# Down products of ten units in three feed-forwards as float32r passes, with their low parts made by GpSimd

## The chip, the core and the metric

One Trainium2 chip, one of its cores. The metric is the device time of one launch in microseconds, first to last instruction plus a little around it. Three runs of the kernel before gave 507.08, 507.49 and 510.03 us, median 507.49.

## What is computed

Sixteen sequences of 128 tokens with 256 channels go through two layers. The first is a WKV recurrence over the tokens and then a feed-forward with a product-key mixture of experts beside it; the second is a linear cross attention and then a mixture of eight experts with the best two per token. What the change touches is the first feed-forward, cut from the reference:

```
mlp = silu(x @ gate_w) * (x @ up_w) @ down_w          # 256 -> 1024 -> 256
ew  = silu(einsum('nh,nkh->nk', x, de)) * softmax(scores)
experts_states = einsum('nk,nkh->nh', ew, ue)         # 512 experts, 8 chosen by keys
x = x + tanh(g_ffn[0]) * (mlp + experts_states)
```

## The kernel before

All 2048 tokens stay in SBUF. They are worked on in four groups of four sequences (512 tokens, `GN`). Each group has one feed-forward, ("mlp", 0) to ("mlp", 3), here called the first to the fourth. A feed-forward has twelve units of 128 hidden rows: eight of the dense part and four of the experts of the product keys. For each unit TensorE makes the hidden rows (`block_up`: for a dense unit banks A and B, six float32r matmuls of 512 columns each, since the product of two float32 values is made as low times high, high times low, high times high), ScalarE takes Silu of A into the ring `act_s` of four buffers, VectorE multiplies with B, and TensorE multiplies the result with the unit's rows of `w_down` (`down`, L678: four token tiles, one float32 matmul of 256 columns each, added up in the two banks `acc`). A float32 matmul stands in the trace as two records, a float32r matmul as one.

The order of the whole program is one list, `SCHED`, written by hand, and every engine walks it in the same order and does its share of each step. A feed-forward has the parts 1 to 13 (and the downs of units 10 and 11 as parts 14 and 15); part p makes the hidden rows of unit p-1 and the down product of unit p-4 (`LAG` is 3), and after it stand the steps of other work that the table `PLAN` gives for that part: the recurrence of later groups (`wkv_in`, `wkv_out`), keys and values of the attention (`kv_k`, `kv_e`, `kv_v`), the routing of the experts (`route`), and from the third feed-forward on the attention (`attn`) and the second layer's experts (`moe`, `place`, `rows`, `send`). No engine goes past an instruction that waits. TensorE takes the six PSUM banks `ring` in turn, so it can run ahead of the engines that empty them by six banks.

Places that matter below. The step `clear` of the second feed-forward's part 12: after the last keys GpSimd zeroes a row in `v_t0`, and SyncE copies it over the tensors `x_rows` in HBM by two large DMAs (L1756, semaphore `rows_cleared`). The step `send`: GpSimd scatters rows that ScalarE scaled (`rows`, L1158) by indirect DMAs (L1677), two per tile. `wkv_out 3 3` and `3 5`: GpSimd multiplies with the reciprocals of VectorE (L1655). Memory is full: the names in `with nc.sbuf_tensor(...)` and `pass` are second names for words of what is allocated behind them.

## Time and profile before

| | |
|---|---|
| median of 3 runs | 507.49 us |
| profiled execution | 508.22 us |
| its span, first to last instruction | 506.4 us |
| granted TensorE clock, mean | 0.974 of full |
| TensorE, VectorE, ScalarE, GpSimd busy | 89%, 69%, 49%, 34% |
| first feed-forward's downs begin | 66 us |
| third and fourth feed-forward | about 207 to 385 us |

The span is 1.8 us shorter than the time of the same execution; that rest lies around the program. The engines of the table overlap, so their shares don't add. Stages are told apart by the start of the down products: those of the second feed-forward run from 144.8 to 206.4 us, those of the third from 221.8 to 298, those of the fourth from 319 to 384. In a timeline a row may hold several instructions of one kind ("x8"); the bracket at its end is the idle time of the engine before it and what ended that.

### The profile page before, as it was taken

To read this page: it belongs to the slowest core of one execution; us is meant where nothing else is said; L and a number is where in the kernel's file an instruction comes from. 1 tells how busy PE (TensorE), PEld (TensorE's weight loads), DVE (VectorE), ACT (ScalarE), POOL (GpSimd) and SP (SyncE) were. 2 spreads that over 40 slices of the span, in tenths; PEclk is the share of its full clock that TensorE was granted. 3 is DMA by queue.
4 is the path that set the end of the run, shared out by engine and by line. 5 is a ranking of instruction groups with operands and counts; after the bars stand their busy time and mean duration, and the time that the engine had idled before them with its cause. 6 is when DMAs were issued, how large, how long until landed. Compare 5 with 4: busy or idle time off the path is not lost. (4 is left out here: it accounts for less than half of the span.)

```text
span 506.4 us, 7287 instructions
## 1 busy us (share of the span) xinstructions
PE 450.3 (89%) x2162; PEld 356.1 (70%) x2162; DVE 347.2 (69%) x994; ACT 247.2 (49%) x479; POOL 173.8 (34%) x181
## 2 busy tenths in 40 slices
PE   2769799589989999999999998998998899899991
PEld 1447588458668776888778786887776688788860
DVE  6968569988486964577978967888778354621173
ACT  2868264223577377455044416360751544955540
POOL 3787232354022333400000000060525015477771
PEclk9999799789999999999999999999999899999997
DMA  8421212002000000980000000142323223346494
GB/s 306 164 80 57 62 33 80 5 20 83 1 1 2 0 1 0 293 218 0 1 2 1 0 2 0 32 136 74 119 71 112 88 79 111 105 150 191 123 380 138
DMA packets 32966, 42.02 MB, mean 83 GB/s; under 512 B 3483, under 2 KB 26781, under 8 KB 32928
## 3 DMA queue, kind: packets, MB, share of 16 engines
q1 hardware_dynamic: 28224, 32.28, 21.0%
q0 software_dynamic: 3744, 8.42, 4.5%
q10 hardware_dynamic: 960, 0.86, 0.5%
q8 instruction: 19, 0.31, 0.3%
q14 instruction: 19, 0.16, 0.1%
HBM read 24.97 MB, written 18.39 MB: 86 GB/s over the span
## 5 line engine op out<-in xcount | busy, mean ns | idle before, releaser
L678 PE MATMUL acc<-w_down,act_s 128*128 128x256 f32 x384 | 91.5, 384 | 0.9 <-DVE act_s L1410 0.9
L678 PEld LDWEIGHTS acc<-w_down,act_s 128*128 128x128 f32 x384 | 73.6, 193 | 12.8 <-DVE act_s L1410 1.3
L654 PE MATMUL ring<-xt_h,up_l 128*128 128x512 f32 x160 | 71.1, 444 | 1.4 <-DVE kv_sum L1490 1.4
L1137 ACT ACTIVATE act_s<-ring 128x512 f32<-128x512 f32 x48 | 28.6, 596 | 73.5 <-PE ring L656 73.3
L655 PE MATMUL ring<-xt_l,up_h 128*128 128x512 f32 x160 | 63.4, 396 | 0.0
L656 PE MATMUL ring<-xt_h,up_h 128*128 128x512 f32 x160 | 63.3, 395 | 0.0
L1625 POOL TENSOR_TENSOR rstd<-var_eps,minus_half 128x4 f32<-128x4 f32 x14 | 14.5, 1039 | 135.7 <-DVE var_eps L1225 135.7
L717 PE MATMUL ring<-up_e,act_s 128*128 x184 | 45.7, 392 | 2.3 <-issue 2.0
L1677 POOL DMA_INDIRECT x_rows<-main_a,slots x32 | 31.1, 972 | 43.7 <-ACT main_a L1158 34.8
L1414 DVE TENSOR_TENSOR act_s<-ring,act_s 128x512 f32<-128x512 f32 x32 | 21.9, 686 | 34.3 <-ACT act_s L1137 16.4
L717 PEld LDWEIGHTS ring<-up_e,act_s 128*128 128x128 f32 x184 | 34.2, 196 | 7.2 <-issue 3.2
L654 PEld LDWEIGHTS ring<-xt_h,up_l 128*128 128x128 f32 x160 | 30.6, 191 | 9.3 <-issue 2.0
L649 PE MATMUL ring<-small,xn 128*128 128x128 f32 x144 | 20.7, 290 | 18.5 <-DVE xn L1240 13.6
L655 PEld LDWEIGHTS ring<-xt_l,up_h 128*128 128x128 f32 x160 | 30.5, 190 | 7.5 <-issue 1.9
L656 PEld LDWEIGHTS ring<-xt_h,up_h 128*128 128x128 f32 x160 | 30.2, 189 | 7.2
L649 PEld LDWEIGHTS ring<-small,xn 128*128 128x128 f32 x144 | 17.5, 149 | 22.0 <-issue 9.3
L1685 POOL DMA_INDIRECT y_rows<-act_s,block_home x16 | 16.3, 1019 | 31.7 <-ACT act_s L1195 27.1
L1218 DVE BATCH_NORM_STATS2 stats<-x_nat 128x6 f32<-128x256 f32 x64 | 22.4, 412 | 4.5 <-DMA x_nat<-in_x 4.2
L1244 DVE SCALAR_TENSOR_TENSOR x_nat<-ring,small,x_nat 128x512 f32<-128x512 f32 x24 | 18.0, 749 | 10.1 <-PE ring L918 7.7
L1137 ACT ACT_TABLE_LOAD x18 | 23.1, 1283 | 0.3
L1567 DVE TENSOR_TENSOR pairs<-ring,pairs 128x256 f32<-128x256 f32 x12 | 5.1, 424 | 25.4 <-ACT pairs L1178 25.4
L1288 DVE RECIPROCAL main_a<-main_a 128x256 f32<-128x256 f32 x12 | 20.0, 1715 | 0.1
(281 smaller groups left out, 1009.6 us busy)
## 6 DMA issues: line engine op xcount, KB each, us to landing
main_b<-x_rows SPq DMA_DIRECT2D x22, 257.0 KB, 3.0
x_rows<-v_t SPq DMA_DIRECT2D x1, 3983.5 KB, 16.1
up_l<-y_rows SPq DMA_DIRECT2D x5, 512.0 KB, 5.9
stage<-in_w_mlp SPq DMA_DIRECT2D x8, 256.0 KB, 2.6
up_e<-in_w_moe SPq DMA_DIRECT2D x8, 256.0 KB, 2.6
x_rows<-v_t SPq DMA_DIRECT2D x1, 1927.5 KB, 22.4
x_nat<-in_x SPq DMA_DIRECT2D x7, 256.0 KB, 7.9
out_x<-x_nat SPq DMA_DIRECT2D x6, 256.0 KB, 5.0
```

The source lines that it names most:

```text
L649: last = pe.transpose(bank[:, t * P:(t + 1) * P], xn[n % 2][:, t, c * P:(c + 1) * P], ident)
L654: pe.matmul(out, wl, xh, start=first, stop=False, skip_group_check=True)
L655: pe.matmul(out, wh, xl, start=False, stop=False, skip_group_check=True)
L656: return pe.matmul(out, wh, xh, start=False, stop=final, skip_group_check=True)
L678: last = pe.matmul(acc[t // 2][:, t % 2, :], act_s[n % RING][:, tok], w_down[:, u, :], start=u == 0 and t % 2 == 0, stop=final, skip_group ...
L717: last = pe.matmul(bank[:, j * 2 * P:(j + 1) * 2 * P], x_block_t[n % 2][:, c, j * P:(j + 1) * P], up_e[:, bass.ds(e * UP + c * 2 * P, 2 * ...
L1137: act.activation(act_s[n % RING][:, :], bank[:, :], ACT.Silu).then_inc(free_sem((step, "A", u)), 1)
L1218: last = dve.bn_stats(stats[:, n, t, :], x_nat[:, b, :])
L1244: return dve.scalar_tensor_tensor(out, bank, gates[:, gate:gate + 1], out, ALU.mult, ALU.add)
L1288: last = dve.reciprocal(den, den)
L1414: free((step, "B", u), dve.tensor_tensor(s[:, :], bank[:, :], s[:, :], ALU.mult))
L1677: pool.indirect_dma_start(x_rows[group_of(g)], bass.IndirectOffsetOnAxis(ap=slots[:, t, k:k + 1], axis=0), to_send[n % SENDS], None).then_ ...
```

## The change

In the second to fourth feed-forward the down products of units 0 to 9 become three float32r passes for each token tile: high activations with low weights, high with high, low with high. That needs four new things.

- ScalarE rounds each unit's activations (step `hidden`, placed behind the other work of part u+2): `act_h_first` or `act_h_late`, each of two buffers. GpSimd subtracts them from `act_s` in place (`act_l`).
- In the second feed-forward the weights are split, one unit per part: ScalarE copies them rounded into borrowed words (step `weights`), GpSimd makes of these the low part in place, and ScalarE then rounds `w_down` itself in place (step `rounded`, `w_down_h`).
- The low weights lie in `q_pad`, `gate_pad` and `er_pad` for the second feed-forward. At the third one's part 1 SyncE moves them by three DMAs (step `moved`) to words of `main_b` and `v_odd`.
- New waits: TensorE's down waits for `act_low` and for the weights; ScalarE's first `hidden` of the third feed-forward waits until both clearing DMAs have landed (`rows_cleared`, 32), since `act_h_late` has the words of `v_t`; ScalarE's first attention step waits for the three moves; SyncE's first load of rows waits for the fourth feed-forward's unit 9.

```diff
+        if f in SPLIT_DOWNS and 2 <= part < SPLIT_UNITS + 2:
+            SCHED.append(("hidden", f, part - 2))
...
-        6: "wkv_out 3 0 1",
-        7: "wkv_out 3 2 3",
+        6: "wkv_out 3 0 1, rounded 1 5, weights 1 7",
+        7: "wkv_out 3 2 3, rounded 1 6, weights 1 8",
...
+                if f in SPLIT_DOWNS and u < SPLIT_UNITS:
+                    pe.wait_ge(act_low, split_turn(f, u) + 1)
+                    if f == 1:
+                        pe.wait_ge(down_high, u + 1)
+                    else:
+                        pe.wait_ge(low_moved[u // 4], 16)
+                    for t in range(GT):
+                        tok = slice(t * P, (t + 1) * P)
+                        out = acc[t // 2][:, t % 2, :]
+                        pe.matmul(out, high_rows(f, u)[:, tok], low_of(f, u), start=u == 0 and t % 2 == 0, stop=False,
+                                  skip_group_check=True)
+                        pe.matmul(out, high_rows(f, u)[:, tok], w_down_h[:, u, :], start=False, stop=False,
+                                  skip_group_check=True)
+                        last = pe.matmul(out, act_l[:, n % RING, tok], w_down_h[:, u, :], start=False, stop=final,
+                                         skip_group_check=True)
+                    last.then_inc(down_done, 1)
+                    return
...
+                    if g == 0 and c == 0:
+                        for moved in low_moved:
+                            act.wait_ge(moved, 16)
...
+                elif kind == "hidden":
+                    n = unit_of(g, part)
+                    hidden_made(act, n)
...
+                    if g == 2 and part == 0:
+                        act.wait_ge(rows_cleared, 32)
+                    if part >= 2 or g == 3:
+                        act.wait_ge(down_done, n - 1 if part >= 2 else unit_of(g - 1, SPLIT_UNITS + part - 2) + 1)
+                    act.activation(high_rows(g, part), act_s[n % RING][:, :], ACT.Copy).then_inc(act_high, 1)
...
+                    act.activation(first_low(u), w_down[:, u, :], ACT.Copy).then_inc(down_rounded, 1)
+                elif kind == "rounded":
+                    u = part
+                    act.wait_ge(down_low, u + 1)
+                    act.wait_ge(down_done, u + 1)
+                    act.activation(w_down_h[:, u, :], w_down[:, u, :], ACT.Copy).then_inc(down_high, 1)
...
+                    pool.wait_ge(act_high, split_turn(g, part) + 1)
...
+                    pool.wait_ge(down_rounded, u + 1)
```

ScalarE at the start of the third feed-forward, after the routing logits of its part 2 (buffers numbered; `act_s2` is unit 2's Silu). Before:

```order
210 L1137 ACTIVATE act_s1<-ring5 128x512
211 L1079 ACTIVATE logits0<-ring1 128x256
212 L1079 ACTIVATE logits1<-ring1 128x256
213 L1137 ACTIVATE act_s2<-ring2 128x512
214 L1098 ACTIVATE ax_h<-ring4 128x512
215 L1098 ACTIVATE ax_h<-ring5 128x512
```

and the same place now:

```order
239 L1204 ACTIVATE act_s1<-ring5 128x512
240 L1143 ACTIVATE logits0<-ring1 128x256
241 L1143 ACTIVATE logits1<-ring1 128x256
242 L1220 ACTIVATE act_h_late<-act_s0 128x512
243 L1204 ACTIVATE act_s2<-ring2 128x512
244 L1162 ACTIVATE ax_h<-ring4 128x512
245 L1162 ACTIVATE ax_h<-ring5 128x512
```

The rounding of unit 0 (L1220), which has the wait for the cleared rows, now stands ahead of unit 2's Silu and the attention's `ax_h`.

GpSimd in the second feed-forward's parts 6 to 8, before (L1655 is the product with the reciprocals):

```order
70 L1649 TENSOR_TENSOR main_a0<-main_a0,main_b 128x4x128
71 L1655 TENSOR_TENSOR main_a0<-main_a0 128x4x128
72 L1649 TENSOR_TENSOR main_a1<-main_a1,main_b 128x4x128
73 L1655 TENSOR_TENSOR main_a1<-main_a1 128x4x128
```

and now (L1744 is the old L1655, `act_s1` is unit 5, L1762 the low weights):

```order
81 L1757 TENSOR_TENSOR act_l<-act_s0,act_h_first 128x512
82 L1738 TENSOR_TENSOR main_a0<-main_a0,main_b 128x4x128
83 L1744 TENSOR_TENSOR main_a0<-main_a0 128x4x128
84 L1762 TENSOR_TENSOR low_first2<-w_down,low_first2 128x256
85 L1757 TENSOR_TENSOR act_l<-act_s1,act_h_first 128x512
86 L1738 TENSOR_TENSOR main_a1<-main_a1,main_b 128x4x128
87 L1744 TENSOR_TENSOR main_a1<-main_a1 128x4x128
```

Unit 5's low activations stand behind L1744 of the first half and one weight subtraction.

GpSimd in the fourth feed-forward's parts 7 to 9, now (L1776 are the sends, `act_s2` is unit 6); before there was nothing but the `rstd` and the sends:

```order
130 L1757 TENSOR_TENSOR act_l<-act_s1,act_h_late 128x512
131 L1714 TENSOR_TENSOR rstd<-var_eps,minus_half 128x4
132 L1776 DMA x_rows0<-main_a0,slots 3968x257
133 L1776 DMA x_rows0<-main_a1,slots 3968x257
134 L1776 DMA x_rows0<-main_a0,slots 3968x257
135 L1776 DMA x_rows0<-main_a1,slots 3968x257
136 L1757 TENSOR_TENSOR act_l<-act_s2,act_h_late 128x512
```

Unit 6's low activations stand behind the `rstd` of part 8 and four sends.

## Rows read from the trace of the kernel before

**Rows 1.** The page: busy time of each engine.

```profile
PE 450.3 (89%) x2162; PEld 356.1 (70%) x2162; DVE 347.2 (69%) x994; ACT 247.2 (49%) x479; POOL 173.8 (34%) x181
```

**Rows 2.** Stretches: us, then PE, PEld, DVE, ACT, POOL busy, clock, DMA share, GB/s.

```profile
120.00:198.00 78.00, 76.00 (x341) 57.80 (x340) 58.68 (x131) 45.79 (x76) 18.65 (x19) 1.00 0.00 1
198.00:295.00 97.00, 93.63 (x470) 76.45 (x469) 70.94 (x236) 40.77 (x64) 9.60 (x12) 1.00 0.24 67
295.00:385.00 90.00, 85.20 (x408) 67.47 (x408) 70.73 (x255) 41.59 (x89) 24.54 (x25) 1.00 0.21 67
```

**Rows 3.** Timeline of TensorE: one light part, and short matmuls of the fourth feed-forward.

```profile
251.02 0.40 PE L656 MATMUL ring<-xt_h,up_h 128*128 128x512 f32 x1
...
253.12 0.40 PE L656 MATMUL ring<-xt_h,up_h 128*128 128x512 f32 x1
253.35 1.89 PE L678 MATMUL acc<-w_down,act_s 128*128 128x256 f32 x8
...
367.37 1.85 PE L929 MATMUL ring<-later,xt_f_pad 128*128 128x8 f32 x16
```

**Rows 4.** Groups of instructions by form: busy us, mean ns of one, idle before.

```profile
L1590 POOL TENSOR_TENSOR up_l<-stage,up_h 128x512 fp32r<-128x512 f32 x8 | 10.8, 1347 | 11.2 <-ACT up_h L977 11.1
L1631 POOL TENSOR_TENSOR k_e<-k_e,k_r 128x256 f32<-128x256 f32 x8 | 6.0, 748 | 34.8 <-ACT k_e L1052 34.8
```

**Rows 5.** ScalarE in the second feed-forward: one stretch, and its timeline.

```profile
134.00:147.00 13.00, 12.52 (x52) 8.68 (x51) 7.44 (x17) 12.86 (x24) 1.45 (x2) 1.00 0.00 1
...
134.43 0.36 ACT L1047 ACTIVATE k_e<-ring 128x256 f32<-128x256 f32 x1
134.69 0.38 ACT L1048 ACTIVATE k_r<-ring 128x256 f32<-128x256 f32 x1
...
150.72 0.40 ACT L1056 ACTIVATE kv_sum<-ring 128x272 f32<-128x272 f32 x1 [3.62 <-PE ring L793]
```

**Rows 6.** Timeline of VectorE, second feed-forward.

```profile
142.40 0.69 DVE L1414 TENSOR_TENSOR act_s<-ring,act_s 128x512 f32<-128x512 f32 x1 [1.61 <-ACT act_s L1137]
...
160.57 0.69 DVE L1414 TENSOR_TENSOR act_s<-ring,act_s 128x512 f32<-128x512 f32 x1 [1.26 <-ACT act_s L1137]
161.29 5.66 DVE L1276 TENSOR_TENSOR_SCAN main_b<-decay,main_a 128x516 f32<-128x516 f32 x4
```

**Rows 7.** Durations of the scans over the whole run: min/median/max ns.

```profile
L1276 DVE TENSOR_TENSOR_SCAN main_b<-decay,main_a x12: 1205/1232/2258, 11.9 to 164.7; 128x516 f32<-128x516 f32 x12
```

**Rows 8.** GpSimd's product with the reciprocals, and unit 5's down of the second feed-forward.

```profile
171.87 1.30 POOL L1655 TENSOR_TENSOR main_a<-main_a 128x512 f32<-128x512 f32 x1 [6.00 <-DVE main_a L1288]
174.56 1.89 PE L678 MATMUL acc<-w_down,act_s 128*128 128x256 f32 x8
```

**Rows 9.** The clearing DMAs: issues, and KB and us to landing.

```profile
L1756 SPq DMA_DIRECT2D x_rows<-v_t x2: 381/4422/8464, 202.6 to 203.0; - x2
...
x_rows<-v_t SPq DMA_DIRECT2D x1, 1927.5 KB, 22.4
```

**Rows 10.** Timeline at the third feed-forward's start: ScalarE, then TensorE.

```profile
215.55 0.66 ACT L1079 ACTIVATE logits<-ring 128x256 f32<-128x256 f32 x2 [1.69 <-PE ring L817]
216.95 0.60 ACT L1137 ACTIVATE act_s<-ring 128x512 f32<-128x512 f32 x1 [0.74 <-PE ring L656]
221.83 1.89 PE L678 MATMUL acc<-w_down,act_s 128*128 128x256 f32 x8
```

**Rows 11.** Fourth feed-forward: first and last send of part 8, unit 6's down.

```profile
359.07 1.04 POOL L1677 DMA_INDIRECT x_rows<-main_a,slots  x1 [0.20 <-ACT main_a L1158]
362.94 0.96 POOL L1677 DMA_INDIRECT x_rows<-main_a,slots  x1 [0.30 <-issue]
360.96 1.89 PE L678 MATMUL acc<-w_down,act_s 128*128 128x256 f32 x8
```

**Rows 12.** First feed-forward: the stretch after a long idle time, and that idle time.

```profile
94.60:101.40 6.80, 5.93 (x14) 4.46 (x15) 6.66 (x9) 1.51 (x3) 1.83 (x2) 0.50 0.01 2
...
95.47 0.77 PE L744 MATMUL ring<-exps_t_l,sel_exps 128*128 128x512 f32 x1 [5.44 <-DVE exps_t_l L1385]
```

More of the change, by code:

```diff
@@ L203 @@
     gather 0 4 5, blk 0 26, moe 3 1, shared 3 0 1, fetch_tile 1 0 1 2 3, gather_tile 1 0 1 2 3"""
+SPLIT_DOWNS = (1, 2, 3)
+SPLIT_UNITS = 10
 SCHED = steps(START)
@@ L410, in build @@
         up_e = sb("up_e", [P, UPS])
+        with nc.sbuf_tensor("w_down_h", [P, MLP_UNITS, D], F32R) as w_down_h:
+            pass
         w_down = sb("w_down", [P, MLP_UNITS, D])
@@ L479, in build @@
         down_done = sem("down_done")
+        act_high = sem("act_high")
+        act_low = sem("act_low")
+        down_rounded = sem("down_rounded")
+        down_low = sem("down_low")
+        down_high = sem("down_high")
+        low_moved = [sem(f"low_moved{k}") for k in range(3)]
         acc_free = sem("acc_free")
@@ L1142, in _ @@
                             act.activation(host_s[:, 0, :], bank[:, :], ACT.Copy).then_inc(free_sem((step, "EY")), 1)
+                elif kind == "hidden":
+                    n = unit_of(g, part)
+                    hidden_made(act, n)
+                    if g == 1 and part == 0:
+                        for p in range(2):
+                            full(act, (("wkv_out", 1), "Y", p))
+                    if g == 2 and part == 0:
[3 more added lines that the diff above has]
+                    act.activation(high_rows(g, part), act_s[n % RING][:, :], ACT.Copy).then_inc(act_high, 1)
+                elif kind == "weights":
+                    u = part
+                    if u == 0:
+                        for p in range(2):
+                            full(act, (("wkv_out", 1), "Y", p))
+                    act.activation(first_low(u), w_down[:, u, :], ACT.Copy).then_inc(down_rounded, 1)
+                elif kind == "rounded":
+                    u = part
+                    act.wait_ge(down_low, u + 1)
+                    act.wait_ge(down_done, u + 1)
+                    act.activation(w_down_h[:, u, :], w_down[:, u, :], ACT.Copy).then_inc(down_high, 1)
                 elif kind == "moe":
@@ L1664, in _ @@
                                        ALU.subtract).then_inc(qg_low, 1)
+                elif kind == "hidden":
+                    n = unit_of(g, part)
+                    pool.wait_ge(act_high, split_turn(g, part) + 1)
+                    pool.tensor_tensor(act_l[:, n % RING, :], act_s[n % RING][:, :], high_rows(g, part).bitcast(F32),
+                                       ALU.subtract).then_inc(act_low, 1)
+                elif kind == "weights":
+                    u = part
+                    pool.wait_ge(down_rounded, u + 1)
+                    pool.tensor_tensor(first_low(u), w_down[:, u, :], first_low(u).bitcast(F32),
+                                       ALU.subtract).then_inc(down_low, 1)
                 elif kind == "clear":
@@ L1716, in load_pair @@
                 sent(sp, grp)
+                if n == 0:
+                    sp.wait_ge(down_done, unit_of(NG - 1, SPLIT_UNITS - 1) + 1)
                 if n >= 4:
@@ L1760, in _ @@
                     sp.dma_start(w_shared_down, io["w_moe"][0][:, UP:]).then_inc(shared_loaded, 16)
+                elif kind == "moved":
+                    if part == 0:
+                        sp.wait_ge(down_low, SPLIT_UNITS)
+                        sp.wait_ge(y_ready, C * NG)
+                        sp.dma_start(low_home0[:, :].bitcast(F32).rearrange("p (c s n) -> p c s n", c=C, s=2)[:, :, 0, 0:2 * D],
+                                     low_first0[:, :, :].bitcast(F32).rearrange("p (c u) d -> p c (u d)", c=C)).then_inc(low_moved[0], 16)
+                    elif part == 1:
+                        full(sp, (("kv_k", NG - 1), "K", GT - 1))
+                        sp.dma_start(low_home1[:, :, :].bitcast(F32), low_first1[:, :, :].bitcast(F32)).then_inc(low_moved[1], 16)
+                    else:
+                        full(sp, (("query", NG - 1), "Q"))
+                        sp.dma_start(low_home0[:, GT * PAD:GT * PAD + 2 * D].bitcast(F32),
+                                     low_first2[:, 0:2, :].bitcast(F32).rearrange("p u d -> p (u d)")).then_inc(low_moved[2], 16)
                 elif kind == "expert":
```

31 lines of the change are left out of this document (30 added, 1 removed), and 20 rows, old and new, of the table PLAN.

## The prediction

> **What bounds the kernel now.** I read the busy times first, then the stretches, then the timelines of the stretches that the change touches. TensorE is busy 89% of the span and no other engine over 69% [rows 1]; from 120 to 385 us, where the three changed feed-forwards lie, it is busy 97%, 97% and 95% of each stretch at the full clock [rows 2]. There fewer TensorE microseconds are worth their full length, and every new wait of TensorE costs its full length. VectorE is busy 73 to 79% there, ScalarE 42 to 59%, GpSimd 10 to 27%. So engine time for the new work exists on average; the question is whether it can be had at the right moment, because each engine keeps the order of the list.
>
> **The matmuls.** A down of one unit is 8 records. They take 1.89 us with the last one's tail of some 0.38, so 0.216 us each and 1.73 us per unit [rows 3]. The new one is 12 float32r matmuls of 256 columns, which the trace does not have. From above: float32r matmuls of 512 columns start (253.12 - 251.02) / 9 = 0.233 us apart [rows 3], so at most that. From below: matmuls of only 8 columns still start about 0.11 us apart (1.85 less a tail of 0.26, by 15, [rows 3]), since each loads 128 columns of weights. Against 0.216 of a float32 record, float32r has 0.018 extra; half of 0.216 and that extra make 0.126, which I take: it is nearest to the lower row. The new down is 12 x 0.126 = 1.51 us, 0.22 less; 30 units give 6.5 us. By the ends it would be 12 x 0.11 = 1.32 (12 us saved) and 12 x 0.233 = 2.80 (32 us lost). Where a down is set by a wait of another engine its saving is lost; I count 25 units, -5.5 us.
>
> The Trainium skill, TensorE: Matmul & The Clock Gate, sections Back-to-back issue gap and LDWEIGHTS, gives 262 cycles for 256 columns (109 ns at 2.4 GHz) and columns by 1.2 GHz for a weight load (107 ns). By that the new down would be 1.31 us and the saving about 12 us. The trace's float32r rows of 512 columns lie 18 ns above what the page gives for that width, so I keep the rows' number.
>
> **The new work.** ScalarE copies of 256 columns follow each other 0.26 us apart [rows 5], of 512 columns by twice that. Each of the parts 3 to 8 of the second feed-forward gets one of 512 and two of 256, 1.05 us, and a little for their waits: 1.2 us. GpSimd gets 1.35 us per unit and 0.75 us per weight subtraction [rows 4], 30 x 1.35 + 10 x 0.75 = 48 us on an engine that has the room.
>
> **Second feed-forward.** From 134 to 147 us ScalarE is busy without a gap [rows 5], and again from 150.7 to 160: keys, table loads and Silu follow one another. There VectorE's products wait for Silu, at 142.40 and 160.57 [rows 6]. Part 1 gets 0.6 us, part 2 1.2. So the product at 142.40 comes 1.8 us later, and with it the chain through VectorE's statistics and GpSimd that TensorE, and so ScalarE at 150.72 [rows 5], waits for: +2. Parts 4 and 5 add 1.2 each, so the Silu ahead of the product of 160.57, and that product, come 4.4 us later. From there to 177 VectorE is full: four scans 5.66 us [rows 6], then the reciprocals that GpSimd waits for [rows 8]. A scan takes 1.23 us as a rule and up to 2.26 [rows 7], the long ones beside GpSimd's tensor work, of which there is now more in this stretch: +1.3 us. GpSimd's product of 171.87 [rows 8] ends then at 171.87 + 5.7 + 1.30 = 178.9. Behind it stand one weight subtraction and unit 5's low part: 178.9 + 0.75 + 1.35 = 181.0. Unit 5's down began at 174.56 [rows 8]. TensorE is held +6.4 us at this place, the earlier +2 included. The second half (unit 6) follows at the same distance, so nothing is added. After it ScalarE has gaps of over a microsecond per part and the rest is covered. From below this is +2 (if the low part came in time); from above +8.
>
> **Start of the third feed-forward.** The clearing DMAs are issued from 202.6 on and the second, issued at 203.0, lands 22.4 us later: 225.4 [rows 9]. ScalarE's rounding of unit 0 waits for it. Its place in the order is behind the logits, which end at 216.2 [rows 10]. ScalarE so stands from 216.2 to 225.5, and Silu of unit 2 comes at 226.0 in place of 216.95: +9.1. Everything queued on ScalarE behind it comes as late: `ax_h`, the routing exponentials, unit 3's Silu, the attention's exponentials. VectorE's product of unit 2 waits for that Silu and the routing follows it without a gap; what VectorE gives ScalarE for the routing comes some 8 us later, and unit 3's Silu and the attention +8.4 with one more rounding. On TensorE the down of 221.83 waits for the low part (225.5 + 0.5 + 1.35 = 227.4) and for the first move, which queues behind the same clearing traffic: +5.7. Then its two roundings and the attention's chain hold it to +9. The trigger of the clearing is ScalarE's last keys, so all of this moves with the +6.4 and isn't covered by it. Term: +9; from below +5.7, from above +11.
>
> **Fourth feed-forward.** Unit 6's low part stands behind four sends, 359.07 to 363.9 at 1.27 us each with the gap [rows 11]: 364.2 + 1.4 = 365.7, against a down that began at 360.96 [rows 11]. +4.7 us; from below +3, if the rows come earlier against TensorE. Units 7 to 9 come behind fewer sends and later downs: nothing more.
>
> **Clock and port.** After 5.44 us of idle TensorE before 95.47 us the granted clock was 0.50 (1.2 GHz) from 94.6 to 101.4 [rows 12]. The three holds are as long as that or nearly. In the half clock the other engines' chains set the pace in part; I count 2 us, between 0 and 7. VectorE's instructions that GpSimd holds up in the third and fourth feed-forward: 1 us, between 0 and 5. The Trainium skill, SBUF — State Buffer, tells of an exclusive lock: a VectorE instruction with two SBUF inputs stands still for the whole of a GpSimd one. The spread of the scans [rows 7] agrees; in full it would be nearer the upper end here.
>
> **Sum.** Profiled execution 508.2 (span 506.4 and 1.8 around it) - 5.5 + 6.4 + 9.0 + 4.7 + 2 + 1 = 525.8. That execution is 0.7 above the median of 507.5, so 525 us.
>
> **Rivals.**
> - The low parts come in time: TensorE runs three parts behind the hidden rows, and in most parts that is 8 us or more. Then only the matmuls count: 507.5 - 6.5 = 501. This is the side of faster. It holds only if ScalarE's wait for the cleared rows is covered, and [rows 9, 10] speak against it: 9 us between the place and the landing. 7%.
> - Only the clearing wait bites; ScalarE's and GpSimd's additions are swallowed by slack in the second and fourth feed-forward: 507.5 - 6.5 + 9 = 510, with the +2 that is sure 512. For it: mean loads are low [rows 2]. 22%.
> - Short float32r matmuls cost as much as long ones, 0.233: 32 us instead of -6.5 on TensorE, part of it inside the holds, so about 525 + 28 = 553. Against it: float32 matmuls and transposes scale with their columns. 9%.
> - By the page's pace of 0.109 the saving is 10 us at 25 units in place of 5.5, and the same holds give 520. As a mechanism here: the weight load alone sets the pace. 10%.
>
> My forecast has 52%, with a range of its own of 517 to 536. The range that holds 8 in 10 goes from 510 to 539: down to the second rival, not to the first nor the third. About 1% (5 us) is what a measurement of this kernel tells from no change. Faster by over 1%: 0.07. Within 1%: 0.1 (the lower half of the second rival). Slower: 0.83.
>
> **What would show it.** The down's record group at 1.5 us per unit; ScalarE idle 9 us before the first rounding of the third feed-forward with the DMA to `x_rows` as what ended it; TensorE idle before the downs of unit 5 (second), unit 0 (third), unit 6 (fourth feed-forward) ended by GpSimd's `act_l`; stretches at clock 0.50 behind them. The forecast is wrong if TensorE's idle time in the three feed-forwards grows by less than 8 us, or if the downs' pace isn't between 0.11 and 0.14.

## The result: 542 us, slower, and outside the range

Five runs of the changed kernel took 539.76 to 548.11 us, median 542.42; five of the kernel before, on the same chip, 505.56 to 510.03, median 507.08. The ratio is 1.065, its 95% interval 1.060 to 1.071. Forecast were 525 us and a range of 510 to 539: the sign is right, half of the size is missing. Run again beside other kernels it took 543.58 us, a ratio of 1.069 (1.062 to 1.076).

The profiled execution is the slowest of the five, 548.1 us, span 546.3. It has two stretches of 3.4 us more at half clock, at 29 and 40 us, ahead of anything that was changed, and so its first down begins 3.3 us later than in the kernel before (69.5 for 66.2 us). Where I compare the two traces I take that off. From the first changed unit on, the rows of the repeated run (span 541.5) tell nearly the same.

The page of the changed kernel, busy time of each engine, against [rows 1]:

```profile
PE 458.5 (84%) x2282; PEld 366.1 (67%) x2282; DVE 361.8 (66%) x994; ACT 268.8 (49%) x529; POOL 222.1 (41%) x221
```

VectorE has as many instructions as before, 994, and is busy 14.6 us longer. That became the main finding.

Now the three feed-forwards, each from its first down to that of the next (the last one to the down of its unit 11). Columns: from and to, length, busy time of TensorE, of its weight loads, VectorE, ScalarE, GpSimd, granted clock, DMA share, GB/s. First the kernel before:

```profile
144.80:221.80 77.00, 74.24 (x351) 58.01 (x350) 56.33 (x115) 45.04 (x74) 24.79 (x27) 1.00 0.26 73
221.80:319.00 97.20, 93.19 (x462) 75.19 (x461) 75.94 (x267) 39.39 (x58) 4.03 (x4) 1.00 0.04 10
319.00:382.20 63.20, 60.30 (x289) 47.87 (x287) 50.94 (x179) 29.84 (x73) 20.55 (x21) 1.00 0.29 91
```

and the changed one:

```profile
148.60:241.60 93.00, 76.35 (x391) 59.71 (x390) 59.13 (x106) 54.24 (x99) 43.70 (x43) 0.92 0.29 84
241.60:347.60 106.00, 95.20 (x500) 78.55 (x501) 84.59 (x280) 46.89 (x70) 18.75 (x15) 0.95 0.00 1
347.60:423.30 75.70, 62.67 (x330) 51.87 (x328) 54.92 (x177) 33.74 (x81) 31.39 (x29) 0.91 0.25 76
```

Together 237.4 us became 274.7. TensorE is busy 227.7 of the first and 234.2 of the second: its idle time grew from 9.7 to 40.5 us, by 31 (to 39.2 in the repeated run, by 29), where the forecast has 20 us of holds and 1 of stretched VectorE work. It is busy longer although the passes are shorter, because part of its work now runs at the lower clock: the mean fell from 1.00 to 0.92, 0.95 and 0.91. Each of the seven stretches at 1.2 GHz in it lies in or behind an idle time of TensorE of 2.5 us or more.

Where TensorE and ScalarE stand: rows of the changed kernel's timeline, with the idle time and what ended it in the bracket.

```profile
155.10 0.74 PE L857 MATMUL ring<-v_x,k_e 128*128 128x136 f32 x4 [3.23 <-POOL k_e L1720]
182.12 0.47 PE L808 MATMUL ring<-exps_t_l,sel_exps 128*128 128x512 f32 x1 [3.11 <-issue]
184.59 0.58 PE L731 MATMUL acc<-low_first,act_h_first 128*128 128x256 f32 x1 [0.75 <-POOL act_l L1757]
239.37 0.63 ACT L1220 ACTIVATE act_h_late<-act_s 128x512 fp32r<-128x512 f32 x1 [10.46 <-DMA x_rows<-v_t]
241.60 0.55 PE L731 MATMUL acc<-low_home,act_h_late 128*128 128x256 f32 x1 [6.92 <-DMA low_home<-low_first]
280.64 1.10 PE L696 MATMUL ring<-small,xn 128*128 128x128 f32 x8 [2.58 <-DVE xn L1329]
343.15 0.58 PE L701 MATMUL ring<-xt_h,up_l 128*128 128x512 f32 x1 [3.38 <-DVE kv_sum L1579]
375.57 0.77 PE L982 MATMUL ring<-wo,q_pad 128*128 128x256 f32 x1 [4.66 <-DVE q_pad L1539]
398.73 0.58 PE L731 MATMUL acc<-low_home,act_h_late 128*128 128x256 f32 x1 [4.95 <-POOL act_l L1757]
```

The rows of 239.37, 241.60 and 398.73 are the three holds of the forecast, which has 9.3, 5.7 and 4.7 us for them. The others are not in the forecast; three of them (280.64, 343.15, 375.57) wait for VectorE. At 182.12 "issue" is a wrong name: the matmul reads `exps_t_l`, and VectorE ended that just then. VectorE's own timeline says why:

```profile
168.07 0.69 DVE L1503 TENSOR_TENSOR act_s<-ring,act_s 128x512 f32<-128x512 f32 x1 [2.39 <-ACT act_s L1204]
168.80 7.19 DVE L1365 TENSOR_TENSOR_SCAN main_b<-decay,main_a 128x516 f32<-128x516 f32 x4
...
175.91 0.66 DVE L1503 TENSOR_TENSOR act_s<-ring,act_s 128x512 f32<-128x512 f32 x1
...
177.39 3.37 DVE L1377 RECIPROCAL main_a<-main_a 128x256 f32<-128x256 f32 x2
...
180.67 0.63 DVE L1503 TENSOR_TENSOR act_s<-ring,act_s 128x512 f32<-128x512 f32 x1
181.33 0.69 DVE L1474 TENSOR_TENSOR exps_t_l<-ring,exps_t_h 73x512 fp32r<-73x512 f32 x1
```

ScalarE's roundings stand ahead of Silu, so VectorE's product waits for Silu and comes late (168.07). The four scans behind it take 7.19 us in place of 5.66, beside GpSimd's subtractions. Then come the next product (175.91), the reciprocals, and behind them the small thing that TensorE is waiting for. I had followed this chain to GpSimd's low part (181.0 us in the forecast); it passes through VectorE's `exps_t_l` first, and the low part costs only 0.75 us more.

The new instructions, as groups of the changed kernel (form, count, busy us, mean ns, idle time before them):

```profile
L735 PE MATMUL acc<-w_down_h,act_l 128*128 128x256 f32 x120 | 35.4, 295 | 0.0
...
L1757 POOL TENSOR_TENSOR act_l<-act_s,act_h_late 128x512 fp32r<-128x512 f32 x20 | 26.2, 1317 | 50.5 <-ACT act_h_late L1220 50.3
...
L1220 ACT ACTIVATE act_h_late<-act_s 128x512 fp32r<-128x512 f32 x20 | 12.5, 627 | 17.9 <-DMA x_rows<-v_t 10.5 <-PE acc L735 7.3
```

GpSimd's 1.32 us is nearly the forecast's 1.35. The last row holds a wait that I had not named: with two buffers for the high parts, ScalarE's rounding of unit u waits for TensorE's down of unit u-2, 7.3 us in four places.

Taken one by one in their order, 15 of VectorE's 994 instructions are longer by more than 0.1 us than in the kernel before, and they make up 14.3 of the 14.6 us. The largest piece is an instruction of the routing, 128x32 elements, in the changed kernel's timeline of the fourth feed-forward, with GpSimd beside it.

```profile
370.28 3.19 DVE L1451 TENSOR_TENSOR exps<-exps,r_z 128x32 f32<-128x32 f32 x1
...
370.93 2.49 POOL L1757 TENSOR_TENSOR act_l<-act_s,act_h_late 128x512 fp32r<-128x512 f32 x2
...
374.06 1.41 DVE L1539 SCALAR_TENSOR_TENSOR q_pad<-gate_pad,ring 128x512 f32<-128x512 f32 x2
```

and the durations of the same instruction in the kernel before (min/median/max ns):

```profile
L1362 DVE TENSOR_TENSOR exps<-exps,r_z x4: 191/194/194, 86.9 to 342.6; 128x32 f32<-128x32 f32 x4
```

0.19 us of work took 3.19 us: it ended at 373.47, 0.05 us after the second of GpSimd's two subtractions. It had begun 0.65 us before the first of them, while GpSimd issued a send; what held it in that time no run separates. Behind it stands `q_pad` of 374.06, and for that TensorE waits at 375.57. So this stop made 3.0 of its 4.66 us of idle time, though TensorE waited for neither low part there.

### The profile page after: what moved, and what is told of

Read it like the earlier page. It is cut to its first block and busy times, and to the rows that moved or that the text cites. A ratio compares the mean times of both kernels' runs of the same rounds, so it can differ in the third digit from the quotient of the medians.

```text
span 546.3 us, 7689 instructions
## 1 busy us (share of the span) xinstructions
PE 458.5 (84%) x2282; PEld 366.1 (67%) x2282; DVE 361.8 (66%) x994; ACT 268.8 (49%) x529; POOL 222.1 (41%) x221
## 5 line engine op out<-in xcount | busy, mean ns | idle before, releaser
L701 PE MATMUL ring<-xt_h,up_l 128*128 128x512 f32 x160 | 72.8, 455 | 4.1 <-DVE kv_sum L1579 3.4
L702 PE MATMUL ring<-xt_l,up_h 128*128 128x512 f32 x160 | 65.5, 410 | 0.0
L703 PE MATMUL ring<-xt_h,up_h 128*128 128x512 f32 x160 | 65.2, 407 | 0.0
L1757 POOL TENSOR_TENSOR act_l<-act_s,act_h_late 128x512 fp32r<-128x512 f32 x20 | 26.2, 1317 | 50.5 <-ACT act_h_late L1220 50.3
L781 PE MATMUL ring<-up_e,act_s 128*128 x184 | 44.2, 382 | 2.3 <-issue 2.1
L1776 POOL DMA_INDIRECT x_rows<-main_a,slots x32 | 31.7, 990 | 33.7 <-ACT main_a L1247 24.9
L701 PEld LDWEIGHTS ring<-xt_h,up_l 128*128 128x128 f32 x160 | 32.1, 201 | 12.6 <-DVE kv_sum L1579 3.5
L742 PE MATMUL acc<-w_down,act_s 128*128 128x256 f32 x144 | 35.2, 394 | 1.5 <-DVE act_s L1499 1.5
L735 PE MATMUL acc<-w_down_h,act_l 128*128 128x256 f32 x120 | 35.4, 295 | 0.0
L731 PE MATMUL acc<-low_home,act_h_late 128*128 128x256 f32 x80 | 23.9, 299 | 11.9 <-DMA low_home<-low_first 6.9
L742 PEld LDWEIGHTS acc<-w_down,act_s 128*128 128x128 f32 x144 | 28.2, 198 | 6.2 <-DVE act_s L1499 1.9
```

What stands on the lines that cost most here:

```text
L701: pe.matmul(out, wl, xh, start=first, stop=False, skip_group_check=True)
L702: pe.matmul(out, wh, xl, start=False, stop=False, skip_group_check=True)
L703: return pe.matmul(out, wh, xh, start=False, stop=final, skip_group_check=True)
L731: pe.matmul(out, high_rows(f, u)[:, tok], low_of(f, u), start=u == 0 and t % 2 == 0, stop=False, skip_group_check=True)
L735: last = pe.matmul(out, act_l[:, n % RING, tok], w_down_h[:, u, :], start=False, stop=final, skip_group_check=True)
L742: last = pe.matmul(acc[t // 2][:, t % 2, :], act_s[n % RING][:, tok], w_down[:, u, :], start=u == 0 and t % 2 == 0, stop=final, skip_group ...
```

## The experiments

The kernel before ran beside each set, with medians of 508.6, 509.0, 508.5 and 508.1 us, so times of different sets can be compared to within about a microsecond. The changed kernel stands at 543.6, by its repeated run (`e0_again`):

> The changed kernel as it is, beside the others of this set on one chip: 540 to 544 us. It shows how far the stretches at half clock move from run to run; every time of this set is read against it.

The kernels of one set have four runs or more each. Differences of 2 to 3 us between two of them are at the edge of what they show.

### One part of the change alone

The passes alone (`e3_passes_only`). VectorE writes its product rounded into `act_l`, and all three passes read that.

```diff
-                        pe.matmul(out, high_rows(f, u)[:, tok], low_of(f, u), ...
-                        pe.matmul(out, high_rows(f, u)[:, tok], w_down_h[:, u, :], ...
+                        pe.matmul(out, act_l[:, n % RING, tok], w_down_h[:, u, :], ...
+                        pe.matmul(out, act_l[:, n % RING, tok], w_down_h[:, u, :], ...
                         last = pe.matmul(out, act_l[:, n % RING, tok], w_down_h[:, u, :], ...
```

> Left out: the low parts of the activations and of the weights, their moves, and the waits for them; the three float32r passes all read the same rounded product and the same rounded weights, so this is the matmul part of the change alone (with ScalarE's ten roundings of the weights). Theory A (the matmuls cost what the records show, 12 at 0.117 us against 8 at 0.216 us a unit, 0.33 us less; nothing else in this variant holds TensorE): 30 units by 0.33, some 498 us, and 501 at the pace of the forecast. Theory B (short float32r matmuls cost more than they save where TensorE draws instructions and weights): 507 or more.

Measured: 506.09 us, ratio 0.995 (0.990 to 0.999). The same three stretches in its profile:

```profile
145.40:223.10 77.70, 73.07 (x393) 58.55 (x392) 55.85 (x118) 47.90 (x83) 24.77 (x27) 0.98 0.26 71
223.10:319.50 96.40, 90.67 (x502) 74.94 (x501) 75.82 (x265) 39.45 (x58) 4.03 (x4) 1.00 0.04 11
319.50:381.60 62.10, 57.51 (x330) 47.50 (x329) 50.88 (x179) 29.76 (x73) 20.72 (x21) 1.00 0.30 92
```

TensorE is busy 221.2 us in place of 227.7, and about 1.7 of that comes of one stretch of 3.4 us at the lower clock: the passes do save 0.3 us a unit. But the three stretches together are only 1.2 us shorter (236.2 for 237.4), since its idle time grew from 9.7 to 15.0. TensorE's saving is real and most of it is waited away: in units 0 to 4 of the third and fourth feed-forward the downs begin no earlier against before from unit to unit, so the other engines set the pace there, though TensorE was 95 to 96% busy in these two stretches before; it is now 91 to 93% busy.

Everything but the passes (`e4_side_work_only`): one float32 product in their place, with all waits and side work left as they are.

```diff
+                        last = pe.matmul(acc[t // 2][:, t % 2, :], act_s[n % RING][:, tok],
+                                         w_down_h[:, u, :].bitcast(F32), ...
```

> Left out: the three float32r passes; the down products stay one float32 product with the rounded weights' words, while all the new work of ScalarE, GpSimd and SP and all waits stay (GpSimd's low part goes into the high part's words). Theory A (the whole loss is waits, roundings and their consequences, and the passes only save): 542 plus the 7 to 10 us that the passes saved, less what was lost inside the holds: 545 to 552. Theory B (the passes themselves cost, by a slower TensorE or by clock stretches that come of them): 530 or less.

Measured: 546.28 us, ratio 1.075 (1.066 to 1.085). The passes are worth 2.7 us here too, and the side work costs 38 us by itself. Theory A holds; its 7 to 10 us for the passes don't.

### GpSimd's low parts: the queue or VectorE

Cut to 8 of 512 columns (`e7_short_low`), with the third pass reading the high part again, everything else kept:

```diff
-                    pool.tensor_tensor(act_l[:, n % RING, :], act_s[n % RING][:, :], high_rows(g, part).bitcast(F32),
+                    pool.tensor_tensor(act_l[:, n % RING, 0:8], act_s[n % RING][:, 0:8],
+                                       high_rows(g, part)[:, 0:8].bitcast(F32), ...
```

> Left out: GpSimd subtracts 8 of the 512 columns of each low part of the activations, and the third pass reads the high part again. All waits, roundings and passes stay. Theory A (GpSimd's own time, 30 low parts of 1.32 us, queues TensorE's low parts and slows VectorE beside it): 6 us or more less than the changed kernel, above all before unit 5 of the second and unit 6 of the fourth feed-forward. Theory B (GpSimd's length doesn't count; what counts is what stands ahead of it, on ScalarE, VectorE's reciprocals and the sends): 1 to 4 us less, about one low part of 1.3 us for each of the two or three holds that it ends.

Measured: 528.74 us, ratio 1.041 (1.034 to 1.048), 14.8 us less than the changed kernel. On its page VectorE is back near its old time:

```profile
PE 449.9 (86%) x2282; PEld 359.4 (69%) x2282; DVE 348.1 (66%) x994; ACT 268.7 (51%) x529; POOL 190.8 (36%) x221
```

Theory B, which was mine, gave it 1 to 4 us. TensorE's three waits for VectorE shrink from 2.58, 3.38 and 4.66 us to 0.7, 1.4 and 1.6, and its distance to the kernel before, which in the changed kernel grows there by 2.7, 3.5 and 5.7 us, does not grow there at all. The next run tells GpSimd's queue from what it does to VectorE. Zeros are written twice in place of the subtraction (`e9_filled_low`):

```diff
-                    pool.tensor_tensor(act_l[:, n % RING, :], act_s[n % RING][:, :], high_rows(g, part).bitcast(F32),
-                                       ALU.subtract).then_inc(act_low, 1)
+                    pool.memset(act_l[:, n % RING, :].bitcast(F32), 0.0).then_inc(filled, 1)
+                    pool.wait_ge(filled, split_turn(g, part) + 1)
+                    pool.memset(act_l[:, n % RING, :].bitcast(F32), 0.0).then_inc(act_low, 1)
```

> Left out: the low parts of the activations; in place of each subtraction GpSimd fills the same words with zeros twice (0.53 us each by the setup's rows of that shape), so that it is busy about as long (1.1 to 1.3 us) but reads nothing. Everything else stays. With the subtractions cut to 8 columns the kernel had taken 528.7 us. Theory A (GpSimd's reading instruction stops VectorE's: VectorE's busy time of 361.8 us had come down to 348.1): VectorE's busy time is near 348 us and the time 529 to 533. Theory B (GpSimd's time in its own queue holds TensorE's low parts): near 543 us whatever VectorE does. Theory C (any GpSimd instruction stops VectorE, reading or not): VectorE's busy time stays at 358 us or more.

Measured: 532.83 us, ratio 1.048 (1.041 to 1.054), and on its page:

```profile
PE 455.2 (86%) x2274; PEld 363.9 (68%) x2282; DVE 349.1 (66%) x994; ACT 268.7 (50%) x529; POOL 213.6 (40%) x251
```

GpSimd is busy 213.6 us, nearly as long as in the changed kernel (222.1), and VectorE runs free at 349.1. Of the 14.8 us, 10.8 come from VectorE being stopped and 4 from GpSimd's queue: theory A. The fills take 1.06 us where the subtraction took 1.35 on average, so the queue's share is somewhat more. In the traces, from the end of the first feed-forward to the last down, the two shares are 11 and 6 us.

The low parts on VectorE itself (`e10_low_on_vector`):

```diff
+                    dve.wait_ge(act_high, split_turn(g, part) + 1)
+                    dve.tensor_tensor(act_l[:, n % RING, :], act_s[n % RING][:, :], high_rows(g, part).bitcast(F32),
+                                      ALU.subtract).then_inc(act_low, 1)
```

> Changed: VectorE makes the low parts of the activations in place of GpSimd, at the same place of the order; nothing is left out. 30 instructions of about 0.69 us, the price of VectorE's subtractions of that shape, are 20.7 us more on VectorE, against the 14 us by which GpSimd's subtractions had stretched it. Theory A (the lock between the two engines is what costs; VectorE's own 0.69 us a unit costs less than 1.32 us of lock): 3 to 8 us less than the changed kernel. Theory B (VectorE's waits for ScalarE's rounding at that place hold its queue): equal or slower, up to 10 us.

Measured: 532.04 us, ratio 1.046 (1.039 to 1.052): 11.5 us better than by GpSimd, more than expected. VectorE's busy time is 368.0 us, 6 more than in the changed kernel, with 30 instructions more: at 0.70 us each they are the whole of its growth over the kernel before, 20.8 us, so nearly nothing is left of the stops. The busier engine gives the faster kernel. That run frees GpSimd's queue too, so the two gains are not told apart by it.

### The two holds that were forecast

The start of the third feed-forward, by other words for the high parts of two units (`e1_other_words`):

```diff
+            if f == 2 and u < 2:
+                return act_h_two[:, u, :]
...
-                    if g == 2 and part == 0:
+                    if g == 2 and part == 2:
                         act.wait_ge(rows_cleared, 32)
```

> Changed: units 0 and 1 of the third feed-forward keep their high part in other words, so ScalarE's wait for the cleared rows moves from part 2 to part 4; the move of the low parts still queues behind the clearing DMAs. Theory A (the hold at the start of the third feed-forward is ScalarE's wait for rows_cleared, 10.5 us, and what queues behind it): ScalarE's idle time there goes, and 535 us or less comes out of 542. Theory B (TensorE is held by the move of the low weights, whose landing at 241.6 doesn't change): TensorE still waits some 7 us for the move before unit 0's down and the time is 538 to 542. Theory C (the time comes from GpSimd's and VectorE's load, not from this wait): within 2 us of 542.

Measured: 540.75 us, ratio 1.066 (1.057 to 1.074). TensorE's wait for the moves stays, as theory B has it:

```profile
L735 PE MATMUL acc<-low_home,act_h_two 128*128 128x256 f32 x8 | 2.9, 365 | 5.6 <-DMA low_home<-low_first 5.6
```

With the split begun at unit 2 (`e8_from_unit_two`; units 0 and 1 have one float32 product) TensorE's wait and ScalarE's for the cleared rows are out of the way. ScalarE's first attention step still waits for the moves:

```diff
-        if f in SPLIT_DOWNS and 2 <= part < SPLIT_UNITS + 2:
+        if f in SPLIT_DOWNS and (4 if f == 2 else 2) <= part < SPLIT_UNITS + 2:
```

> Changed: units 0 and 1 of the third feed-forward have one float32 product (with the rounded weights' words, so their weights' low parts are left out); the split begins at unit 2, and with it ScalarE's wait for the cleared rows and TensorE's for the moves. Theory A (the hold at the start of the third feed-forward, 10.5 us of ScalarE and 7 us of TensorE, goes through to the end): 7 to 10 us less than the changed kernel, and in the trace the distance to the kernel before doesn't grow between the end of the second feed-forward and unit 0 of the third. Theory B (the wait turns up again at unit 2, or the slack behind it would have taken it up): 0 to 4 us less.

Measured: 537.93 us, ratio 1.060 (1.053 to 1.067). Unit 0 of the third feed-forward comes 6 us earlier against the repeated run of the changed kernel, but against the kernel before 2.9 us are lost again up to unit 2, since the attention waits:

```profile
241.17 1.28 ACT L1178 ACT_TABLE_LOAD   x1 [2.54 <-DMA low_home<-low_first]
```

Net 5.7 us, between the theories. The hold was real and as long as forecast; its worth at the end is two thirds of it.

The fourth feed-forward with `hidden` ahead of the part's other steps (`e2_ahead_of_sends`):

```diff
+        if f == 3 and 2 <= part < SPLIT_UNITS + 2:
+            SCHED.append(("hidden", f, part - 2))
         if part in PLAN[("mlp", f)]:
             SCHED += steps(PLAN[("mlp", f)][part])
```

> Changed: in the fourth feed-forward the step that makes a unit's high and low part stands ahead of the part's other steps, so GpSimd makes the low part before its sends, and ScalarE the high part before its other work. Theory A (TensorE's 4.95 us of idle time before unit 6's down is the low part behind four sends, and the half clock behind it costs about 3 us more): that idle row goes and 536 us comes out of 542. Theory B (the wait moves into another place, since ScalarE's and GpSimd's other steps come later by as much): 540 to 543.

Measured: 534.23 us, ratio 1.054 (1.043 to 1.064), 9.3 us less, twice the term of the forecast. The edit removes two holds: unit 6's, and most of that for `q_pad`, which now reads

```profile
366.10 1.97 PE L984 MATMUL ring<-wo,q_pad 128*128 128x256 f32 x8 [1.85 <-DVE q_pad L1541]
```

against 4.66 us before the same product above: the routing's `exps` takes 0.19 us again, and only one subtraction falls beside its neighbour `r_sum` (1.20 us in place of 0.18).

### ScalarE's two buffers, and the clock

Four buffers in the third feed-forward (`e5_four_buffers`):

```diff
+            if f == 2 and u % 4 < 2:
+                return act_h_two[:, u % 2, :]
...
+                    if g == 2:
+                        if part >= 4:
+                            act.wait_ge(down_done, n - 3)
```

> Changed: in the third feed-forward four buffers in place of two for the high parts, so ScalarE's rounding of unit u waits for the down of unit u-4, not u-2. The wait for the cleared rows stays. Theory A (ScalarE's 7 us of idle time before its roundings, ended by TensorE's downs, hold the attention and the gates, and so TensorE, by 2 to 4 us): the time falls by 2 to 5 us against the changed kernel, and TensorE's rows that wait for er_pad and q_pad in the third feed-forward go. Theory B (ScalarE has time to spare there): within 1.5 us of it.

Measured: 540.80 us, ratio 1.065 (1.058 to 1.072): 2.8 us less, inside theory A's range. The two intervals overlap, so it is likely and not shown.

Zeros multiplied where TensorE would stand (`e6_kept_busy`):

```diff
+            def keep_busy(count):
+                for _ in range(count):
+                    pe.matmul(acc[0][:, 0, :], nothing[:, 0:P], nothing[:, :], start=False, stop=False, ...
```

> Added: matmuls of 256 columns of zeros (float32r), which add nothing to the sums, where TensorE would stand: 24 before the exponentials' spreading in the second feed-forward, 52 before the down of unit 0 of the third, 36 before the attention's output and 38 before the down of unit 6 in the fourth. At 0.117 us each they last about as long as the waits (2.8, 6.1, 4.2, 4.4 us). Theory A (the stretches at half clock follow from TensorE's idle time and cost about 13 us in the three feed-forwards): the four stretches of 6.8 us there go and the time falls by 6 to 10 us. Theory B (in the half clock other engines set the pace, as I had counted): the stretches go, the time stays within 2 us. Theory C (the clock falls for another reason than idle time): the stretches stay.

Measured: 541.32 us, ratio 1.064 (1.058 to 1.071), 2.3 us less. The stretch of the fourth feed-forward from 366 to 412 us, in this kernel:

```profile
366.00:412.00 46.00, 43.62 (x263) 36.64 (x263) 33.49 (x110) 19.27 (x46) 20.31 (x18) 0.96 0.27 81
```

and in the changed kernel's run of the same set:

```profile
366.00:412.00 46.00, 35.22 (x176) 28.16 (x175) 31.34 (x96) 16.36 (x37) 18.04 (x17) 0.89 0.23 73
```

The clock follows the idle time (0.96 for 0.89, and no stretch at half clock is left at the start of the third feed-forward). Yet the time hardly follows the clock: some 3.5 us in the fourth feed-forward, nothing in the other two, where the zeros also came 3.5 us in the way of unit 5. Nearly theory B. Idle time alone does not settle the clock: an idle time of 2.57 us at 278 us has a half-clock stretch of 3.4 us behind it in this run, and the same idle time of the changed kernel has one in its first profile and none in the repeated run's. In a half-clock stretch the others' chains set the pace, as the forecast had it in part.

### All together, and what is left

Short low parts (the third pass reads the high part again), the split from unit 2, and `hidden` ahead in the fourth (`e11_together`, the three edits above in one kernel), of which one line of each:

```diff
+        if f == 3 and 2 <= part < SPLIT_UNITS + 2:
+        if f in SPLIT_DOWNS and f < 3 and (4 if f == 2 else 2) <= part < SPLIT_UNITS + 2:
+                    pool.tensor_tensor(act_l[:, n % RING, 0:8], act_s[n % RING][:, 0:8],
```

> All three suspects taken away at once: the low parts are 8 columns long (the third pass reads the high part again), the split of the third feed-forward begins at unit 2 (units 0 and 1 with rounded weights), and in the fourth the step that makes the parts stands ahead of the part's other steps. ScalarE's roundings, the moves and the weights' low parts stay. Theory A (these three are all but a few us of the loss): 510 to 516 us. Theory B (the second feed-forward's roundings on ScalarE, which stay, cost more than the 4 us that I give them): 517 us or more.

Measured: 515.60 us, ratio 1.016 (1.007 to 1.024). The three take away 28.0 us; singly they were 14.8, 5.7 and 9.3, together 29.8. So they are nearly separate causes, and most of the loss.

Without the weights' low parts as well (`e13_no_weights`):

```diff
-        1: "mlp_out 0 0, route 1 4, kv_k 2 0, kv_e 2 0, rounded 1 0, weights 1 2",
+        1: "mlp_out 0 0, route 1 4, kv_k 2 0, kv_e 2 0, rounded 1 0",
...
-        1: "mlp_out 1 0, attn_in 0 0, query 3 0, moved 2 0 1 2",
+        1: "mlp_out 1 0, attn_in 0 0, query 3 0",
```

> The version with three suspects taken away (515.6 us), and also without the weights' low parts: ten roundings of 0.40 us on ScalarE and ten subtractions on GpSimd in the second feed-forward, the moves, and the waits for them; the first pass reads the rounded weights. The activations' 28 roundings of 0.62 us on ScalarE stay. Theory A (the weights' part makes the second feed-forward late: +2.1 us before unit 5, and part of the +3 before unit 1): 511 to 513 us. Theory B (the activations' roundings ahead of Silu make it late): 514 us or more. The rest to 506 is the other's.

Measured: 511.57 us, ratio 1.006 (1.003 to 1.010). The weights' part costs 4.0 us. The 5.5 down to 506.1 are put down to the 28 roundings on ScalarE and what waits for them, which is what is left, with the 8-column subtractions and the float32 products of two units; no run takes them away by themselves. In the two profiles, from the end of the first feed-forward to the last down, this kernel is only 2.2 us behind `e3_passes_only`, so where the rest arises is open. That is theory A's size for the weights, but its place only in part: over the second feed-forward the distance to the kernel before grows by 3.8 us in `e11_together` and by 2.1 here, and up to unit 2 of the third by 2.8 us there and 0.4 here. There it is ScalarE's first attention step that waits for the moves (2.46 us in `e11_together`, nothing here), and TensorE behind it.

A complete version with what helped (`e12_vector_four`: low parts by VectorE, four buffers, other words for two units, by the edits above):

```diff
+                    dve.wait_ge(act_high, split_turn(g, part) + 1)
...
+            if f == 2 and u % 4 < 2:
+                return act_h_two[:, u % 2, :]
...
+                    if g == 2 and part == 2:
                         act.wait_ge(rows_cleared, 32)
```

> A complete version, nothing left out: VectorE makes the low parts of the activations; in the third feed-forward four buffers hold the high parts, and units 0 and 1 use the other words, so that ScalarE's wait for the cleared rows moves to part 4. VectorE alone had given 532.0 us, four buffers 3 us less and the other words 3 us less than the changed kernel. Theory A (these add up, as the first causes did): 525 to 528 us. Theory B (TensorE's wait for the moves of the weights takes the place of both): 530 to 532 us. In neither is it faster than before, since the passes alone give only 2.5 us.

Measured: 525.39 us, ratio 1.034 (1.026 to 1.042). The gains add up, and the kernel stays 17 us behind the one before. No version here beats it by more than the 0.5% of the passes alone, which leave out the low parts.

## Why the forecast was short

The ladder of runs, from the kernel before to the changed one, beside the terms of the sum:

| step | forecast | runs |
|---|---|---|
| the passes | -5.5 | 508.5 to 506.1: -2.5 |
| activations' roundings (ScalarE), 8-column low parts | part of +6.4 | to 511.6: +5.5 |
| weights' low parts, moves | part of +6.4 and +9.0 | to 515.6: +4.0 |
| GpSimd's low parts, start of the third, order in the fourth | the rest of +6.4, of +9.0, +4.7, +2, +1 | to 543.6: +28.0 |

- **The matmuls.** The twelve records of one down start between 173.97 and 175.27 us, 0.118 apart:

```profile
173.97 0.28 PE L731 MATMUL acc<-low_first,act_h_first 128*128 128x256 f32 x1
...
175.27 0.28 PE L735 MATMUL acc<-w_down_h,act_l 128*128 128x256 f32 x1
```

  The forecast had 0.126, between 0.11 and 0.233, so the pace was nearly right, and the rival of long matmuls (553) fell at once. What failed is "25 units count", and with it the sentence that fewer TensorE microseconds are worth their full length there: only about a third of the saving reached the end. TensorE's busy share of 97% in [rows 2] is an average; the 3% of idle time sits where the other engines lead, and a faster TensorE only arrives there earlier. By the page TensorE: Matmul & The Clock Gate of the Trainium skill, section Back-to-back issue gap, 256 columns take 109 ns; the trace's 118 lies 9 above.
- **Second feed-forward, +6.4.** In the changed kernel's trace the distance to before has grown by 3.4 us at unit 1 (forecast 2) and by 6.7 at unit 5 (forecast 6.4). The product that was forecast 4.4 us late is 4.2 late, the scans are 1.5 us longer (forecast 1.3). At unit 6 come 2 us more, where the forecast adds nothing; they are gone with the 8-column subtractions. The size is nearly right. The step "GpSimd's product ends, one weight subtraction, unit 5's low part" named the wrong releaser: TensorE waits for `exps_t_l` of VectorE first.
- **Start of the third, +9.0.** ScalarE waited 10.5 us in place of 9.3, TensorE 6.9 in place of 5.7, and at unit 2 the distance had grown by 10. Right in the trace. Worth 5.7 at the end (`e8_from_unit_two`), where the attention's wait for the moves still costs 2.9 up to unit 2.
- **Fourth, +4.7.** 4.95 us of idle time before unit 6: right. But with the edit that removes it 9.3 us go, since its other effect, on `q_pad`, was not in the sum.
- **Clock, +2.** 2.3 us came back where the gaps were filled; of the six stretches of the repeated run three went and one was halved, and two short ones came. Nothing speaks against the size, though there are more stretches than the three I counted; those that stayed are untried.
- **VectorE's instructions held up by GpSimd, +1, between 0 and 5.** This is the step that failed. VectorE's busy time grew by 14.6 us, and taking that away (`e9_filled_low`) gives back 10.8 us. I had priced it by the spread of the scans [rows 7], the long instructions, whose worst case is one microsecond. What decides is not how long VectorE's instruction is but how much of GpSimd's is still to come: one of 0.17 us took 1.29 beside a subtraction of 1.27, one of 0.19 took 3.19. The bound should have been 30 new subtractions times 1.32, about 40 us of stopped VectorE if every one met a victim at its start; about a third of that came. Nor had I looked for which VectorE instructions stand on chains to TensorE: three holds of the third and fourth feed-forward (2.7, 3.5 and 5.7 us in the trace) are not in the sum. The Trainium skill, SBUF — State Buffer, section Who interferes with whom, has the rule that I cited: an exclusive lock, taken by a GpSimd instruction that reads SBUF against a VectorE one with two SBUF inputs, not by one that only writes. The runs agree on both halves: 14.6 us with subtractions, 1.9 with fills of the same place, where the VectorE instructions with two inputs keep their old length. I weighed it as "nearer the upper end"; it lay far beyond the upper end that I had set.
- **Not in the sum at all:** ScalarE's wait for its own two buffers (some 2.8 us by `e5_four_buffers`, likely and not shown).

Of the 17 to 18 us that the forecast lacks, VectorE's stops are some 10, the matmul term 3, and ScalarE's buffers perhaps 3. The rest is not assigned.

The mark that I gave for being wrong, idle time growing by less than 8 us, looked to one side only. It grew by 31.

## To carry over

Price a GpSimd instruction that reads by what it may stop, not by its own queue: look for VectorE's short instructions on chains near it, those with two SBUF inputs first, and for each take GpSimd's full length as the worst case. Where GpSimd's instructions stand back to back, it can be two of them. If the work has to be done, VectorE may do it faster for the kernel even where VectorE is the busier engine. And a saving on an engine that is 97% busy was worth a third of itself here: look at who leads where it idles before counting units.

## What the runs showed that was not expected

- Back-to-back subtractions hold a VectorE instruction now for one of them, now for both. The `exps` of 370.28 ended 0.05 us after the second of two. But each of the two `onehot` instructions here (0.42 us alone) ended 0.28 us after one of the two subtractions, the first of them at 271.35, with the second subtraction running. What decides between the two is open.

```profile
269.80 2.68 POOL L1757 TENSOR_TENSOR act_l<-act_s,act_h_late 128x512 fp32r<-128x512 f32 x2
270.10 2.66 DVE L1436 TENSOR_TENSOR onehot<-iy_b,key_iota 128x512 bf16<-128x512 bf16 x2
```

- Two fills of 128x512 words, 0.53 us each, leave VectorE's busy time almost alone (349.1 us against 348.1 with 8-column subtractions), but not every instruction. Those with two SBUF inputs keep their length beside a fill, such as the two `onehot` of 265.41 in `e9_filled_low`. Some with one tensor input are held: the cast `s_if` takes 1.29 us beside a subtraction and 0.52 beside a fill, in place of 0.17, and an `xn` of 0.40 us takes 0.69 beside the fills. First the changed kernel, then two rows of the other:

```profile
338.92 1.27 POOL L1757 TENSOR_TENSOR act_l<-act_s,act_h_late 128x512 fp32r<-128x512 f32 x1 [7.16 <-ACT act_h_late L1220]
338.93 1.29 DVE L1559 CAST s_if<-s_idx 128x8 f32<-128x8 uint32 x1
...
265.41 0.76 DVE L1437 TENSOR_TENSOR onehot<-iy_b,key_iota 128x512 bf16<-128x512 bf16 x2
...
331.60 0.52 DVE L1560 CAST s_if<-s_idx 128x8 f32<-128x8 uint32 x1
```

- In the fourth feed-forward filling the gaps raised the mean clock of 46 us from 0.89 to 0.96 and gave back some 3.5 us; at the start of the third it took a stretch of 6.8 us at 1.2 GHz away and gave nothing. That suggests that most of what looks like lost clock there is time in which TensorE would have waited.
